# Two attentions of a four-layer model on one core: denominators by token, each head projected by itself

## The reference, cut to what matters

```python
lat = layer_norm(latents, g, b); ctx = layer_norm(context, gc, bc)
q = (lat @ Wq).reshape(b, n, HEADS, 64).transpose(0, 2, 1, 3)
k, v = jnp.split(ctx @ Wkv, 2, axis=-1)            # by head, as q
k = apply_rope(k, cos, sin)
attn = jnp.clip(jnp.einsum('bhnd,bhsd->bhns', q, k) * 64 ** -0.5, -11.0, 11.0)
attn = jax.nn.softmax(attn, axis=-1)
out = jnp.einsum('bhns,bhsd->bhnd', attn, v)
x = x + out.transpose(0, 2, 1, 3).reshape(b, n, 1024) @ Wo + bo
```

## Time and profile before

| what | us |
|---|---|
| median of 3 runs (2813.58 to 2816.3) | 2813.99 |
| the profiled execution, device time | 2822.15 |
| its span, first to last instruction | 2820.4 |
| granted TensorE clock, mean of the span | 0.863 of full |

### The profile page before, as it was taken

How to read it: one execution, slowest core, us unless ns; L and a number is a source line. 1 busy time by engine, 2 the same in 40 slices (tenths; PEclk the granted TensorE clock), 3 DMA queues, 4 the chain that set the end, 5 groups by cost and what they waited for, 6 DMA issues and landing times.

```text
span 2820.4 us, 34532 instructions
## 1 busy us (share of the span) xinstructions
PE 2203.5 (78%) x13832; PEld 1504.2 (53%) x13832; DVE 1384.1 (49%) x2156; ACT 760.7 (27%) x1164; POOL 702.7 (25%) x757
## 2 busy tenths in 40 slices
PE   2788998838967889887796778399768888469994
PEld 2444444328964444433685445299634444358884
DVE  4688777743135666676324444222456554312212
ACT  2433343302113233322111323000124444211111
POOL 3211211123331001100123222255511110154443
PEclk8899999969987888988797777599869999689997
DMA  3010100018950000000382000199400000078883
GB/s 139 16 28 25 30 15 21 14 59 285 311 183 8 8 8 16 11 8 12 116 274 95 22 12 7 50 337 327 156 12 18 10 10 3 20 259 294 296 280 98
DMA packets 96559, 274.66 MB, mean 97 GB/s; under 512 B 14128, under 2 KB 44592, under 8 KB 96016
## 3 DMA queue, kind: packets, MB, share of 16 engines
q0 software_dynamic: 45168, 206.99, 21.2%
q1 hardware_dynamic: 51232, 65.46, 7.4%
HBM read 239.50 MB, written 20.32 MB: 92 GB/s over the span
## 4 chain that ended last, share of the span: by engine, by line
PE 60%; DVE 19%; DMA 7%; issue 6%; POOL 4%; ACT 3%; SPq 0%; POOLq 0%; DVEq 0%; ACTq 0%
PE psum L277 11%; PE psum L1938 11%; PE psum L1961 7%; PE psum L713 7%; PE psum L693 7%; DVE plain L1475 3%; DVE plain L851 3%; DVE plain L824 3%; PE psum L1305 2%; PE psum L1278 2%; DMA plain<-in_l_en,plain 2%; PE psum L1322 2%; PE psum L743 2%; DMA plain<-sorted_x 2%; POOL sorted_x L1866 2%
## 5 line engine op out<-in xcount | busy, mean ns | idle before, releaser
L1938 PE MATMUL psum<-plain 128*128 128x128 f32 x3904 | 493.3, 279 | 10.4 <-DMA plain<-in_l_shared 8.6
L1938 PEld LDWEIGHTS psum<-plain 128*128 128x128 f32 x3904 | 485.5, 196 | 22.5 <-issue 8.7
L277 PE MATMUL psum<-split 128*128 128x256 f32 (+1 forms) x1728 | 397.7, 382 | 67.5 <-DVE split L350 9.8
L277 PEld LDWEIGHTS psum<-split 128*128 128x128 f32 x1728 | 295.1, 214 | 211.9 <-issue 121.6
L2062 POOL DMA_INDIRECT plain<-in_l_ffn,plain x274 | 260.1, 949 | 400.8 <-PE psum L1961 383.9
L990 ACT ACTIVATE plain<-psum 128x1024 f32<-128x1024 f32 x224 | 229.3, 1025 | 421.6 <-PE psum L713 312.9
L1961 PE MATMUL psum<-plain 128*128 128x256 f32 x1160 | 305.2, 386 | 34.7 <-DVE plain L2027 34.7
L693 PE MATMUL psum<-plain 128*64 128x512 f32 x896 | 260.1, 671 | 32.1 <-DVE plain L858 26.3
L851 DVE TENSOR_TENSOR plain<-plain 128x1024 f32<-128x1024 f32 x200 | 265.9, 1330 | 10.0 <-ACT plain L990 7.1
L713 PE MATMUL psum<-split 64*128 64x512 f32 x1536 | 249.3, 439 | 17.3 <-DVE plain L824 16.4
L1018 POOL TENSOR_TENSOR plain<-plain 128x512 f32<-128x512 f32 x48 | 72.5, 1510 | 725.0 <-DMA plain<-plain 721.8
(11 more groups left out here) (176 smaller groups left out, 2278.1 us busy)
## 6 DMA issues: line engine op xcount, KB each, us to landing
plain<-plain SPq DMA_DIRECT2D x192, 64.0 KB, 2.1
plain<-sorted_x SPq DMA_DIRECT2D x76, 128.0 KB, 5.6
sorted_y<-plain SPq DMA_DIRECT2D x76, 128.0 KB, 4.3
plain<-in_l_w SPq DMA_DIRECT2D x20, 256.0 KB, 2.7
plain<-in_l_ffn,plain POOLq DMA_INDIRECT x274, 6.1
plain<-in_ctx SPq DMA_DIRECT2D x8, 512.0 KB, 6.0
plain<-in_l_wo SPq DMA_DIRECT2D x28, 128.0 KB, 2.0
plain<-in_l_tab SPq DMA_DIRECT2D x3, 1024.0 KB, 4.9
```

The costliest lines, as they stand in the source:

```text
L277: m = t.e.matmul(out, lhs[x], rhs[y], start=(first and n == 0), stop=(last and n == 2), skip_group_check=skip)
L1938: m = t.e.matmul(K.bank(b)[:, 256 * z + P * f:256 * z + P * f + P], ws[:, f, c0:c0 + 128], xt[:, k, :], start=(f == 0 and k == 0 and z == ...
```

## The change

`divide` sums by token: eight matmuls for each step, with a 128x128 block of `SA` as the loaded matrix and one column of ones as the moving one, give a 128x8 block of denominators, tokens on the partitions, and VectorE takes the reciprocal of these 128x8 (`K.RCP`). The multiplication of bank 4 goes away: ScalarE copies bank 4 to `OT` undivided (`copied`, a new side item). `output` becomes two items of two 128-token tiles each; in it each head is projected by itself from its 64 rows (a row group) into a bank of its own, eight matmuls in all, and VectorE adds each product times its reciprocal to `x` (`scalar_tensor_tensor`, eight in place of four adds). `divide` and `output` also move: `side64` now runs the first four items of the preparation (two key halves, one quarter of the values where there is one, one split) ahead of `divide`, and the weights of the pace follow this.

```diff
@@ -510,7 +510,7 @@
                 prep += [1.4] + [1.4] * own + [1.4] * len(last) + ([0.5] * 12 + [0.9] if own else [])
-            weights = [0.5] * (n > 0) + prep[:2] + [1.8] * (n > 0) + prep[2:]
+            weights = prep[:4] + [1.9, 1.0, 1.0] * (n > 0) + prep[4:]
             total = max(sum(weights), 1.0)
@@ -546,18 +546,20 @@
 
-def side64(n, A, divide, prepare, output, tail):
-
+def side64(n, A, copied, divide, prepare, output, tail):
+
+    if n:
+        copied(n - 1)
+    g = prepare(n + 1)
+    for _ in range(4):
+        next(g, None)
+        yield
     if n:
         divide(n - 1)
         yield
-    g = prepare(n + 1)
-    for _ in range(2):
-        next(g, None)
-        yield
-    if n:
-        output(n - 1)
-        yield
+        for half in range(2):
+            output(n - 1, half)
+            yield
     yield from g
@@ -720,30 +722,39 @@
         weigh(n, nk - 1)
-        t.emptied_at(4, "divided", K.count("divided", (L, n)))
+        t.emptied_at(4, "av_copied", K.count("av_copied", (L, n)))
 
     def divide(n):
+
         b = RB.get()
         t.bank(b)
         t.wait_ge("ones", 1)
         t.wait_ge(*A.adds[n, nk - 1])
-        for h in range(2):
-            m = t.e.matmul(K.bank(b)[64 * h:64 * h + 64, :], K.ONES, A.SA[n % 2][:, h, :], start=True, stop=True)
+        for i in range(4):
+            for h in range(2):
+                m = t.e.matmul(K.bank(b)[:, 2 * i + h:2 * i + h + 1], A.SA[n % 2][:, h, 128 * i:128 * i + 128],
+                               K.ONES[:, 0:1], start=True, stop=True)
         m.then_inc(*t.up("sums", L, n))
         K.at["sums", L, n] = b
         t.emptied_at(b, "recip", K.count("recip", (L, n)))
 
-    def output(n):
+    def output(n, half):
+
         p = A.steps[n][0]
-        t.wait_ge("divided", (L, n))
+        t.wait_ge("av_copied", (L, n))
         t.wait_ge(f"wo{p % 2}", (L, p))
-        for i in range(4):
-            b = RB.get()
-            t.bank(b)
-            t.e.matmul(K.bank(b)[:, 0:256], A.OT[:, 128 * i:128 * i + 128], K.WO64[p % 2], start=True,
-                       stop=True).then_inc(*t.up("out", L, n, i))
-            K.at["out64", L, n, i] = b
-            t.emptied_at(b, "x_added", K.count("x_added", (L, n, i)))
+        bs = [RB.get(), RB.get()]
+        t.bank(*bs)
+        for i in range(2):
+            q0 = 128 * (2 * half + i)
+            for h in range(2):
+                r = slice(64 * h, 64 * h + 64)
+                m = t.e.matmul(K.bank(bs[h])[:, 256 * i:256 * i + 256], A.OT[r, q0:q0 + 128], K.WO64[p % 2][r, :],
+                               start=True, stop=True)
+        m.then_inc(*t.up("out", L, n, half))
+        K.at["out64", L, n, half] = tuple(bs)
+        for h in range(2):
+            t.emptied_at(bs[h], "x_added", K.count("x_added", (L, n, half, h)))
 
@@ -752,11 +763,12 @@
     for n in range(A.n):
-        side = side64(n, A, divide, prepare, output, tail)
+        side = side64(n, A, nothing, divide, prepare, output, tail)
         attend(n, side)
         run(side, 1000)
     divide(n)
-    output(n)
+    output(n, 0)
+    output(n, 1)
 
@@ -863,22 +875,25 @@
         if n:
-            v.wait_ge("out", (L, n - 1, 3))
+            v.wait_ge("x_added", v.made["x_added"])
         v.wait_ge("sums", (L, n))
-        v.e.reciprocal(A.OT, K.bank(K.at.get(("sums", L, n), 0))).then_inc(*v.up("recip", L, n))
-        v.wait_ge("recip", (L, n))
-        v.wait_ge("weighed", (L, n, nk - 1))
-        v.e.tensor_tensor(A.OT, K.bank(4), A.OT, ALU.mult).then_inc(*v.up("divided", L, n))
-
-    def output(n):
+        v.e.reciprocal(K.RCP[:, 0:8], K.bank(K.at.get(("sums", L, n), 0))[:, 0:8]).then_inc(*v.up("recip", L, n))
+
+    def output(n, half):
         b = A.steps[n][1]
         v.wait_ge("biased", v.seen["biased"])
-        v.wait_ge("x_added", v.made["x_added"] - 4)
-        for i in range(4):
-            v.wait_ge("out", (L, n, i))
-            x = K.X[:, 4 * b + i, :]
-            v.e.tensor_tensor(x, x, K.bank(K.at.get(("out64", L, n, i), 0))[:, 0:256],
-                              ALU.add).then_inc(*v.up("x_added", L, n, i))
+        v.wait_ge("recip", (L, n))
+        v.wait_ge("out", (L, n, half))
+        banks = K.at.get(("out64", L, n, half), (0, 0))
+        for h in range(2):
+            if h or half == 0:
+                v.wait_ge("x_added", v.made["x_added"])
+            for i in range(2):
+                q = 2 * half + i
+                x = K.X[:, 4 * b + q, :]
+                m = v.e.scalar_tensor_tensor(out=x, in0=K.bank(banks[h])[:, 256 * i:256 * i + 256],
+                                             scalar=K.RCP[:, 2 * q + h:2 * q + h + 1], in1=x, op0=ALU.mult, op1=ALU.add)
+                m.then_inc(*(v.up("x_added", L, n, half, h) if i else v.up("x_added")))
 
...
@@ -971,6 +987,13 @@
         s.e.activation(A.QM[n % 2], K.bank(K.at.get(("shifts", L, n), 0)), ACT.Copy).then_inc(*s.up("max_row", L, n))
+
+    def copied(n):
+
+        if n:
+            s.wait_ge("out", (L, n - 1, 1))
+        s.wait_ge("weighed", (L, n, nk - 1))
+        s.e.activation(A.OT, K.bank(4), ACT.Copy).then_inc(*s.up("av_copied", L, n))
 
@@ -1001,9 +1024,10 @@
     for n in range(A.n):
-        side = side64(n, A, nothing, prepare, nothing, tail)
+        side = side64(n, A, copied, nothing, prepare, nothing, tail)
         attend(n, side)
         run(side, 1000)
+    copied(n)
 
...
@@ -1102,7 +1126,7 @@
             if bt == 1 and p + 2 < A.npair:
-                y.wait_ge("out", (L, n - 2, 3))
+                y.wait_ge("out", (L, n - 2, 1))
                 sync_load_out64(y, K, L, p + 2)
 
     sync_load64(y, K, L, 1)

```

7 lines of the change are left out of this document (4 added, 3 removed).

## The result

The changed kernel took 2841.27 us (median of 4 runs, 2836.97 to 2845.38), the kernel before, beside it, 2815.14 us: ratio 1.0102, 95% interval 1.006 to 1.0144. The forecast was 2804 us, range 2790 to 2825. The profiled execution of after is the fastest of the four, 2836.97 us, against 2822.15 before; it shows the loss smaller than the medians do.

A forecast was written before the change was run, and what follows sets the result against it. Neither TensorE nor VectorE was full; they waited for each other, mostly at the seam between steps. First attention -19.9 and second +9.5 made -10.4: profiled 2822.15 to 2811.8, median 8.2 lower, so 2804 us, range 2790 to 2825.

The forecast's parts named there:

- the term of -18.2: First attention, steps 1 to 13: each step falls from 30.8 to 29.4 us, 1.4 less, 18.2 us in all.
- The first rival: Slow clock stays in the first attention: steps of 30.9, the 13 x 1.4 lost, 2823 us; chance 0.22.
- the +9.5 of the second attention: Second attention: sums +6, bunched maxima +3.7, last step's blocks -3.2, end +3; 9.5 us slower.
- The claim that this stall is covered: First attention: TensorE's wait for the second output item's bank, about 17 to 19, is covered by 2.5 us to spare.
- The work in front of the loop: First attention: VectorE loses 5.7 us a step before its exponential, clip and add rounds and gains 4.1, 1.6 less.
- The fourth rival: The reciprocal wasn't the point: the adds the seam waits for stay; first attention -2, 2814 to 2820 us; chance 0.12.
- Step 14: First attention, no values to prepare: both splits ahead of the fourth exponential, 30.1 against 28.6 us, +1.5.
- The open outputs: End of the first attention: sums, outputs and eight scaled adds follow the last blocks' adds uncovered, +4 us.
- The bunching, +3.7: Second attention: maxima as 4, 3, 4, 1 cost 1.13 less 0.4 us in each of five steps, +3.7.
- the third rival: Row groups don't overlap, or VectorE's emptying of banks sets the pace: second attention +11, 2815 us; chance 0.11.
- The second rival: GpSimd and VectorE don't meet in the first attention: steps of 28.4, 2791 us; chance 0.15.
- the 0.9 of the sum: First attention's step: GpSimd's second rotation slows VectorE's clip and add by 1.7 us; about half remains, +0.9.

The follow-up runs named there:

- b_short_recip: Kernel before, first attention's wide reciprocal replaced by one of 128x8 and a multiplication with a table, so the division is left out; ratio to before 0.9994.
- l1_spread: The change in the second attention alone, its maxima spread over the blocks as in the kernel before; ratio to before 1.003.
- late_half: The change in the first attention alone, with the second output item moved behind the second quarter of the values; ratio to before 1.0012.

## Why the prediction was wrong, point by point

**The step that failed** is the comparison in "so 30.8 - 29.4 = 1.4 a step", the term of -18.2. 30.8 was the old step with its slow clock, 29.4 the new one without. The working had split off 1.5 us of slow clock and did not subtract it: 30.8 - 1.5 = 29.3 is the old step at full clock, and 29.2 to 29.8 is what it measures. So the whole gain of 18.2 us hung on the clock staying up. The first rival said what happens if it doesn't, but the sum took the gain as one of VectorE's loop. The clock stayed at 0.95, and the thirteen steps gained 5.1 us. The second step that failed is the +9.5 of the second attention, which measured +24 (below). The new step at full clock, 29.35, was forecast as 29.4, with its waits: the exponential behind line 958 waits for GpSimd (16.7 us in eight steps), and TensorE for line 894, in after's waits over the same eight steps:

```profile
PE psum L752 <- DVE plain L894: 14.8, 8, 3.6
```

The claim that this stall is covered held in the seven of twelve steps with no slow clock behind it, 29.35 to 29.6. In the other five the slow clock came behind it and made 30.9 or more, the number of the first rival, and the mean lies between the two. First scores of steps 1 and 14, before (713), then after (715):

```profile
114.66 0.97 PE L713 MATMUL psum<-split 64*128 64x512 f32 x6
...
514.75 0.96 PE L713 MATMUL psum<-split 64*128 64x512 f32 x6
```

```profile
115.36 0.96 PE L715 MATMUL psum<-split 64*128 64x512 f32 x6
...
510.32 0.96 PE L715 MATMUL psum<-split 64*128 64x512 f32 x6 [0.32 <-issue]
```

That is 400.1 us before and 395.0 after, 30.8 and 30.4 a step.

**"The work in front of the loop", the reciprocal.** The fourth rival, that it wasn't the point, was right in kind (b_short_recip), though its 2814 to 2820 lies 21 us and more under the result; it had 0.12. The earlier trace rows had the sign: 24.1 of VectorE beside 27.4 of TensorE.

**Step 14, the last step and the ends.** Step 14 was put at +1.5; from its first scores to those of the last step (541.16 against 543.24) it took 30.8 us against 28.5, +2.4, with the longest stall before an output item, 4.01 us. The last step's blocks gained 6.0, as forecast (-6.2). The open outputs were put at +4 and cost 7.4. After, in order of time:

```profile
563.67 2.06 PE L735 MATMUL psum<-plain 128*128 128x1 f32 x9
...
565.66 2.08 PE L752 MATMUL psum<-plain 64*128 64x256 f32 x8
...
568.87 2.08 PE L752 MATMUL psum<-plain 64*128 64x256 f32 x8 [1.14 <-DVE plain L894]
...
570.99 1.79 DVE L894 SCALAR_TENSOR_TENSOR plain<-psum,plain 128x256 f32<-128x256 f32 x4 [1.35 <-PE psum L752]
```

The nine last of the sixteen sums alone take 2.06 us. The forecast had the sums at low clock, but not the outputs, nor that the second half waits for the first's banks, in the open. The last pair gained 0 in place of 1. Counted from the first scores of step 1, which came 0.7 us late, the first attention gained 1.4 us, and it ended 0.7 us early, for -19.9.

**Second attention.** Forecast +9.5, measured +24 by medians. The sums' time was right (1.95 us for 2.1). Its price was near: 8.7 us for a microsecond a step, not 6. The bunching, +3.7, was mis-sized: 8. The outputs' split, taken as free, is near 6.5 by two ratios whose intervals overlap. The last two are more than their own time. A likely reason, not shown, is that this part of the kernel runs at a mean clock of 0.9 and that one slow stretch is worth an estimated 1.6 us (TensorE's 28.4 against 26.8 in steps of after with and without one): two steps of l1_spread, 56.2 at 0.94 and 59.7 at 0.89, differ by about two of them. I had given the clock rival to the first attention only. In the profile of after, the last step's blocks gained 2.0 for the 3.2 of the forecast, and the sums and outputs behind them cost 5.3 for 3.

**The rest.** Row groups overlap (1.13 us for a half, 2.27 a step against 1.99 to 2.02 for half as many matmuls before), so the third rival fell in that form. Its other form, VectorE's emptying of the banks as a stall, was seen in the first attention and in the open outputs, not in the inner steps of the second. The second rival, no collision, was wrong: beside GpSimd's second rotation the low part of the keys took 1.30 us and the clip 1.77, against 0.69 each alone, so all of the 1.7 us is there and not the half that I took, and the step was 29.35 nevertheless. So the 0.9 of the sum was too small by 0.8, and something else in it as much too large. VectorE of after, in order of time:

```profile
279.09 1.30 DVE L803 TENSOR_TENSOR split<-plain,split 128x512 fp32r<-128x512 f32 x1 [1.82 <-ACT split L958]
280.31 1.77 DVE L870 TENSOR_SCALAR plain<-plain 128x1024 f32<-128x1024 f32 x1
```

The range ended at 2825, because it held no case in which the first attention's gain was lost and the second attention lost more than 9.5; the third rival had +20.5 for the second, but with the whole gain of the first.

## What to carry to other kernels

Split a step into work at full clock, waits and slow clock, and compare like with like; a gain that consists only of the clock must be called that and given a chance of its own. Look at the engine that waits and give it work there (one item moved, 0.74% here), before making the other engine faster (3.0 us a step removed, nothing gained). Splitting a product over more banks of a short ring can turn slack of the emptying engine into stalls of TensorE, here up to 4.01 us; and a stall taken away at one place can come back at another (late_half).

## What the runs showed of the hardware

Waits of 1.77 and 1.23 us among dense work are enough for the granted clock to fall behind them, in most steps of before (mean 0.95), not in all; with the first of them at 0.20 and no other over 0.9 it stayed at 1.00 for 300 us. The Trainium skill ("TensorE: Matmul & The Clock Gate", "A second HAM failure mode: psum-queue depth-cycling") tells of another kernel in which short idle times between groups of matmuls make the clock go up and down; the traces agree.

The clock fell also behind sixteen matmuls with a 128x128 block as weights and one column, with no wait in the 11 us before them (after at 1194.19), and at other times it did not (l1_spread at 1134.12). One and 64 columns take nearly the same, 1.95 and 2.00 us for sixteen. The Trainium skill ("TensorEngine Tiling (Array Packing)", "Instruction Overhead") says that one column costs as much as sixty, and this agrees. The 0.12 us of each is far over the floor of 60 cycles that the Trainium skill gives there, an estimated 0.025 us at 2.4 GHz. That the weights set it is likely, since one, four and 64 columns on 128x128 weights all cost 0.12 to 0.13 us, but no run changed the weights alone.

The same code of the first attention (that of before) reached its last sums at 568.5 to 583.65 us in different kernels; the two at the ends had 22 and 65 us at the lower clock on the way. A single profile can't tell less than that apart.
